# Third feed-forward weights transformed in the prologue and the first batch instead of the last batch of attention

## What is computed

```python
up_gate = jnp.einsum('bsd,hd->bsh', x, W1)
up_lin = jnp.einsum('bsd,hd->bsh', x, W3)
hidden = jax.nn.silu(up_gate) * up_lin
hidden = fwht(hidden)                      # h = 1, 2, 4 ... 512: (a + b, a - b), scale 1/sqrt(1024)
out = jnp.einsum('bsh,dh->bsd', hidden, W2)
...
x = x + _L0_attn_a_ref(_layernorm(x, axis=-1), ...)
x = x + _L0_ffn_ref(_layernorm(x, axis=-1), W1, W2, W3)
x = x + _L0_attn_b_ref(_layernorm(x, axis=-1), ...)
x = x + _L0_ffn_ref(_layernorm(x, axis=-1), W1, W2, W3)
```

## Time and profile before

| | us |
|---|---|
| median of 3 runs | 581.48 (581.45 to 582.91) |
| the profiled execution | 581.49 |
| its span, first to last instruction | 579.7 |
| prologue, up to the first step of `score_kq` | 0 to 35.4 |
| first, second, third, last batch of attention | 35.4 to 87.3, to 141.8, to 196.4, to 248.5 |
| the rest | 248.5 to 579.7 |

### The profile page before, as it was taken

The page is one execution under the profiler, slowest core; times in us unless marked ns, Lnnn a source line. Parts: engine busy times, 40 slices in busy tenths (PEclk is TensorE's granted clock), DMA queues, the critical chain, the costliest instruction groups (busy, mean ns, idle before and its releaser), DMA issues.

```text
span 579.7 us, 8904 instructions
## 1 busy us (share of the span) xinstructions
PE 560.9 (97%) x3278; PEld 388.5 (67%) x3278; DVE 384.3 (66%) x734; ACT 304.5 (53%) x559; POOL 174.1 (30%) x203
## 2 busy tenths in 40 slices
PE   8999999999999989899999999999999999999997
PEld 5543433354344333288889888888778888888887
DVE  6998888988898898754363544458887436354433
ACT  3668778868876877643334342344445333424221
POOL 4453265453344597411101010023333010101000
PEclk9999999999999999999999999999999999999999
DMA  5367320320132310010000000000000010010101
GB/s 155 101 203 209 113 75 30 126 69 1 57 119 90 146 38 3 2 73 1 1 0 1 1 1 2 1 1 0 1 1 1 1 36 1 0 37 2 36 1 37
DMA packets 17995, 25.74 MB, mean 44 GB/s; under 512 B 3048, under 2 KB 11240, under 8 KB 17568
## 3 DMA queue, kind: packets, MB, share of 16 engines
q1 hardware_dynamic: 16732, 24.10, 12.9%
q10 hardware_dynamic: 1220, 1.07, 0.6%
HBM read 10.89 MB, written 5.24 MB: 28 GB/s over the span
## 4 chain that ended last, share of the span: by engine, by line
PE 82%; DVE 8%; ACT 5%; issue 2%; DMA 1%; POOL 1%; ACTq 1%; SPq 0%; DVEq 0%
PE PS L372 80%; DVE mxr L1042 2%; PE PS L383 2%; DVE ring L1132 1%; DMA qf<-in_wq 1%; ACT xTh L787 1%; DVE PR L1243 1%; ACT xf L787 1%; ACT qf L801 1%; DVE XNs L1023 1%; ACT PR L969 1%; POOL xTl L1274 1%; PE PS L588 1%; DVE AOl L1034 1%; DVE OT L1109 0%
## 5 line engine op out<-in xcount | busy, mean ns | idle before, releaser
L372 PE MATMUL PS<-xTh,ring 128*128 128x512 f32 x608 | 188.7, 392 | 0.0
L1042 DVE TENSOR_REDUCE mxr<-PS 128x1 f32<-128x512 f32 x256 | 163.2, 681 | 24.4 <-PE PS L372 23.9
L906 ACT ACTIVATE PR<-PS 128x512 f32<-128x512 f32 x256 | 138.4, 603 | 41.6 <-PE PS L372 41.4
L372 PEld LDWEIGHTS PS<-xTh,ring 128*128 128x128 f32 x608 | 113.2, 188 | 23.6 <-issue 1.7
L372 PE MATMUL PS<-xTl,ring 128*128 128x512 f32 x304 | 110.3, 391 | 0.4 <-POOL xTl L1274 0.4
L372 PE MATMUL PS<-ring 50*128 50x512 f32 (+1 forms) x512 | 99.4, 451 | 5.7 <-DVE mxr L1042 4.4
L1192 DVE TENSOR_TENSOR PR<-PR,PS 128x512 f32<-128x512 f32 x64 | 43.8, 685 | 90.6 <-PE PS L372 66.2
L787 ACT ACTIVATE AOh<-PR 128x512 fp32r<-128x512 f32 x72 | 45.5, 632 | 101.9 <-DVE PR L1192 89.9
L372 PEld LDWEIGHTS PS<-ring 50*128 50x128 f32 (+1 forms) x512 | 41.4, 184 | 83.3 <-ACT PR L906 56.7
L1034 DVE TENSOR_TENSOR AOl<-PR,AOh 128x512 fp32r<-128x512 f32 x72 | 51.1, 710 | 50.3 <-ACT AOh L787 50.3
L1274 POOL TENSOR_TENSOR xTl<-xf,xTh 128x512 fp32r<-128x512 f32 x30 | 43.3, 1459 | 137.0 <-ACT xTh L787 137.0
(11 more groups left out here) (135 smaller groups left out, 627.1 us busy)
## 6 DMA issues: line engine op xcount, KB each, us to landing
ring<-qh SPq DMA_DIRECT2D x48, 128.0 KB, 2.7
ring<-ql SPq DMA_DIRECT2D x24, 128.0 KB, 2.7
ring<-weight_scratch SPq DMA_DIRECT2D x3, 1024.0 KB, 4.7
weight_scratch<-in_w SPq DMA_DIRECT2D x2, 1024.0 KB, 6.8
X<-in_x SPq DMA_DIRECT2D x3, 512.0 KB, 6.7
out<-X SPq DMA_DIRECT2D x6, 256.0 KB, 2.2
ring<-AOh SPq DMA_DIRECT2D x8, 128.0 KB, 2.8
ring<-AOl SPq DMA_DIRECT2D x4, 128.0 KB, 2.8
```

Source lines behind the costliest of these rows:

```text
L372: return nc.tensor.matmul(dst, lhsT, rhs, start=start, stop=stop, skip_group_check=True)
L906: nc.scalar.activation(PR[:, j % 8, :], PS[:, kq_bank(j), :], ACT.Exp, scale=HD ** -0.5)\
L1042: nc.vector.tensor_reduce(mxr[:, S % 2, blk, TT * p + t:TT * p + t + 1], PS[:, QK0 + i % 3, :], AX.X, ALU.max, negate=True).then_inc(max_d ...
```

## The change

1. SyncE loads all of W2 (1 MB) and the Hadamard matrix right after the first small loads, ahead of the bias loads, into the part of X that batches three and four fill later; their own load now waits for the last butterfly (`fly_done` 5).
2. GpSimd runs the first butterfly stage (X into PR) ahead of the splits of the first q and k, the second (PR into X) right behind the first `split_max`, and the third in step 4 of the first batch (into XNs and xf). ScalarE waits for the second stage ahead of its first exponential, since that overwrites PR.
3. The four Hadamard products stand in steps 18, 22, 24 and 28 of the first batch. ScalarE reads each twice (copy into qf, high part into W2h) and GpSimd subtracts. The second half of the v projection of the second batch goes whole into step 26; GpSimd's normalising of the third batch now waits for the first two products.
4. In the last batch products, butterflies and their splits are gone; GpSimd's `output_lo` goes from step 13 back to step 6.
5. In the prologue the first transpose of maxima moves from the front of unit 9's projection to the end of unit 8's (the ninth unit), and the last filler matmul goes. VectorE takes the second batch's statistics in one piece.

```diff
-HAD_AT = (16, 17, 26, 28)
-FLY_AT = (3, 5, 7, 9, 11)
+HAD_AT = (18, 22, 24, 28)
+V_FIRST_AT = ((20,), (26,))
...
@@ sync: behind the loads of rbias
+            sp.dma_start(X[:, 2 * TT:4 * TT, :], w2.rearrange("(f p) n -> p f n", p=P)).then_inc(w2_in, DMA)
+            sp.dma_start(had[:, :], had_d).then_inc(w2_in, DMA)
             sp.dma_start(bvt[:, :], bv.partition_broadcast(P)).then_inc(const_in, DMA)
...
                     if b == 0 and s == 9:
+                        sp.wait_ge(fly_done, 5)
                         for c in range(2, BATCH):
...
@@ tensor: beside_maxima
-                    if U == 9:
+                    project_v(0, (U - 6) // 2, U % 2, PS[:, V_BANK[(U - 6) // 2], :])
+                    if U == 8:
                         pe.wait_ge(ml_done, 1)
...
-                    project_v(0, (U - 6) // 2, U % 2, PS[:, V_BANK[(U - 6) // 2], :])
...
-                else:
+                elif U == 10:
                     keep_busy(1, PS[:, 0, :], FILL)
@@ tensor: shared_bank
+                        elif b == 0:
+                            pe.wait_ge(w2h_done, 4)
...
-                if not more and s in HAD_AT:
+                if b == 0 and s in HAD_AT:
                     j = HAD_AT.index(s)
                     if j == 0:
                         pe.wait_ge(fly_done, 5)
+                        pe.wait_ge(qk_f, 4)
+                    elif j == 1:
                         pe.wait_ge(mt_ready, turned // 8)
                     elif j == 2:
-                        pe.wait_ge(x_done, 2 * b)
+                        pe.wait_ge(w2h_done, 2)
                     else:
-                        pe.wait_ge(w2h_done if j == 1 else w2l_done, j)
+                        pe.wait_ge(v_copied, 4)
                     mm(MB, had[:, :], fly_half(j // 2)[:, j % 2 * SEQ:(j % 2 + 1) * SEQ], True, True)\
                         .then_inc(had_ready, 1)
...
+                if b == 0 and s == V_FIRST_AT[1][0]:
+                    pe.wait_ge(w2h_done, 3)
+                    for part in range(2):
+                        project_v(1, 1, part)
...
@@ scalar
+            act.wait_ge(fly_done, 4)
             for K in range(STEPS * BATCH):
...
-                if b == BATCH - 1 and s in HAD_AT[:2]:
+                if b == 0 and s in HAD_AT:
                     j = HAD_AT.index(s)
                     act.wait_ge(had_ready, j + 1)
-                    hi(hadamard_part(j), MB, 1.0 / HID ** 0.5)
+                    act.wait_ge(*((qk_lo, 7 + j) if j < 2 else (w2l_done, j - 1)))
+                    hi(qf[:, j % 2, :], MB, 1.0 / HID ** 0.5)
                     hi(W2h[:, 2 * j:2 * j + 2, :].rearrange("p f n -> p (f n)"), MB, 1.0 / HID ** 0.5)\
                         .then_inc(w2h_done, 1)
@@ vector
-                if b == BATCH - 1 and s in [k + 1 for k in HAD_AT[2:]]:
...
-                    nc.vector.scalar_tensor_tensor(l, MB, 1.0 / HID ** 0.5, h.bitcast(F32), ALU.mult, ALU.subtract)\
-                        .then_inc(w2l_done, 1)
@@ gpsimd
+            pool.wait_ge(w2_in, 2 * DMA)
+            for h in range(2):
+                v, w = (u.rearrange("p (m u n) -> p m u n", u=2, n=D) for u in (fly_raw(h), fly_near(h)))
+                fly(v[:, :, 0, :], v[:, :, 1, :], w[:, :, 0, :], w[:, :, 1, :])
             first_lo(2)
             first_lo(3)
             split_max(0)
+            for h in range(2):
+                pool.wait_ge(fly_done, h + 1)
+                v, w = fly_near(h), fly_raw(h)
+                fly(v[:, 0:SEQ], v[:, SEQ:], w[:, 0:SEQ], w[:, SEQ:])
...
+                if K == 4:
+                    pool.wait_ge(lnT_ready, 4)
+                    pool.wait_ge(x_hi, 4)
+                    pool.wait_ge(fly_done, 4)
+                    fly(fly_raw(0), fly_raw(1), fly_half(0), fly_half(1))
...
+                        if b == 0:
+                            pool.wait_ge(had_ready, 2)
```

More of the change, by code:

```diff
@@ L146, in build @@
             sem(n) for n in ("wv_in", "wo_in", "bias_in", "ident_in", "const_in", "ones_in"))
-        w2_in = [sem(f"w2_in{h}") for h in range(2)]
+        w2_in = sem("w2_in")
         one_done, zero_done, vone_done, pool_init, whi_done, wlo_done, wol_done = (
@@ L617, in shared_bank @@
                     else:
-                        pe.wait_ge(w2h_done, 2)
+                        pe.wait_ge(mt_ready, turned // 8)
                     for part in range(2):
@@ L628, in shared_bank @@
                     else:
-                        pe.wait_ge(qk_f, 4)
+                        pe.wait_ge(w2h_done, 1)
                     for part in range(2):
                         project_v(b + 1, 0, part)
-                if s in V_AT[1] and more:
-                    if s == V_AT[1][0] and b:
+                if b == 0 and s == V_FIRST_AT[1][0]:
+                    pe.wait_ge(w2h_done, 3)
+                    for part in range(2):
+                        project_v(1, 1, part)
+                if b and s in V_AT[1] and more:
+                    if s == V_AT[1][0]:
                         pe.wait_ge(x_done, 2 * b)
-                    elif s == V_AT[1][0]:
-                        pe.wait_ge(mt_ready, turned // 8)
                     project_v(b + 1, 1, V_AT[1].index(s))
@@ L800, in qk_evacuate @@
                 act.wait_ge(qk_lo, 4 * b + n - 1)
+                if b == 2 and n < 2:
+                    act.wait_ge(w2l_done, 3 + n)
                 nc.scalar.activation(qf[:, n % 2, :], MB, ACT.Identity, bias=bqk[:, n:n + 1]).then_inc(qk_f, 1)
@@ L919, in _ @@
                     for half in range(2):
-                        if s == V_AT[half][-1]:
+                        if s == (V_AT if b else V_FIRST_AT)[half][-1]:
                             v_evacuate(b + 1, half)
-                if b == BATCH - 1 and s in HAD_AT[:2]:
+                if b == 0 and s in HAD_AT:
                     j = HAD_AT.index(s)
                     act.wait_ge(had_ready, j + 1)
-                    hi(hadamard_part(j), MB, 1.0 / HID ** 0.5)
+                    act.wait_ge(*((qk_lo, 7 + j) if j < 2 else (w2l_done, j - 1)))
+                    hi(qf[:, j % 2, :], MB, 1.0 / HID ** 0.5)
                     hi(W2h[:, 2 * j:2 * j + 2, :].rearrange("p f n -> p (f n)"), MB, 1.0 / HID ** 0.5)\
@@ L1083, in _ @@
             dve.wait_ge(x_in[1], DMA)
-            for t in range(2):
-                tile_statistics(TT + t, TT + t)
+            for t in range(TT):
+                last = tile_statistics(TT + t, TT + t)
+            last.then_inc(bst_done, 1)
             stack_rows(0)
             stack_rows(1)
-            for t in range(2, TT):
-                last = tile_statistics(TT + t, TT + t)
-            last.then_inc(bst_done, 1)
             moments(TT, TT, 2)
@@ L1388, in _ @@
                     divide(K // 8 - 1)
-                if s == (13 if b == BATCH - 1 else 6) and b:
+                if s == 6 and b:
                     output_lo(2 * b)
@@ L1404, in _ @@
                        WOh[:, :, :].rearrange("p g n -> p (g n)")).then_inc(wol_done, 1)
[L1405 to L1429 removed]
+                if K == 4:
[3 more added lines that the diff above has]
+                    fly(fly_raw(0), fly_raw(1), fly_half(0), fly_half(1))
+                if b == 0 and s in [k + 1 for k in HAD_AT]:
                     j = HAD_AT.index(s - 1)
                     pool.wait_ge(w2h_done, j + 1)
[L1432 removed]
+                    lo(W2l[:, 2 * j:2 * j + 2, :].rearrange("p f n -> p (f n)"), qf[:, j % 2, :],
                        W2h[:, 2 * j:2 * j + 2, :].rearrange("p f n -> p (f n)")).then_inc(w2l_done, 1)
```

44 lines of the change are left out of this document (4 added, 40 removed).

## The result

| | median of runs, us | lowest to highest | profiled execution | its span | TensorE's clock in it |
|---|---|---|---|---|---|
| before | 582.19 (4 runs) | 581.45 to 582.91 | 581.49 | 579.7 | 1.00 |
| changed | 578.12 (4 runs) | 577.90 to 578.27 | 578.27 | 576.4 | 1.00 |

The ratio is 0.9932 with a 95% interval of 0.9916 to 0.9948: faster by 4.1 us, more than the 0.3% that counts here. The forecast was 578.7. Between the two profiled executions it is 3.2 us.

What follows compares the result with a forecast made beforehand. TensorE, busy 97% of the span, was taken as the bound, so time could come only from its waits. Terms -0.5 + 3.1 - 5.4 = -2.8 us took 581.5 to 578.7 us, range 577.2 to 580.6.

Steps and rivals of the forecast that it cites:

- Part 1: Prologue: the earlier transpose of maxima starts step 0 0.5 us sooner, -0.5 us, bounds 0 and 0.9.
- VectorE allows 0.4 to 0.5: Prologue: VectorE, taking 20 maxima in 13.16 us without a gap, leaves room for a 0.4 to 0.5 us gain.
- The cover for the butterflies: Prologue: W2 lands at 16, GpSimd's idle time from 19.2 hides the butterflies, cost 0.
- the broad reading of the port rule: Prologue: VectorE and GpSimd always exclude each other, so eight butterflies hold maxima up by as much as 10 us.
- Part 2: First batch: four added products cost 4.4 us, waits of 1.31 absorb part, +3.1 us, bounds 2.4 and 4.4.
- step 28's small wait: First batch: step 29's transpose waits about 0.4 us for step 28's copy, given back by small gaps ahead of transposes.
- rival A: First batch: shared-bank hand-overs and ScalarE's copies delay exponentials and eat the gain, 581.0 or half, 580.0; chance 0.20.
- Each pair stands between two steps' exponentials: First batch: ScalarE's two copies per product, about 0.55 us each, fit between exponentials, except in step 28.
- Part 3: Last batch: without products, maxima and then ScalarE's exponentials pace it, -5.4 us, bounds -3.9 and -6.0.
- Rival D: First and last batch: TensorE's 4.4 us only change place, only waits go, 578.5; shares chance 0.58 with the forecast.
- Rival B: Prologue: late W2 delays GpSimd's butterflies, costing us for us from a landing at 22, 584.2 at 27.5; chance 0.04.
- the risk 2 in 100: Whole kernel: gaps in TensorE's work drop its clock to half rate; chance 2 in 100.

Runs made afterwards that it cites:

- e1: Kernel before with only the transpose of maxima moved behind unit 8's projection and the last filler removed: 582.38 us median, ratio 0.9993.
- e3: Changed kernel with the four first-batch Hadamard products and ScalarE's copies of them cut to 8 columns: 575.54 us.
- e7: Changed kernel with the four products at full size and only ScalarE's copies of them cut to 8 columns: 577.54 us.
- e9: Changed kernel with the last product in step 27 instead of 28: 577.83 to 578.64 us at full clock (seven executions), three slower up to 585.22.
- e2: Kernel before without the last batch's four Hadamard products, their copies and splits: 576.15 us.
- e5: Kernel before with one unused Hadamard product added ahead of TensorE's long wait in step 28 of the last batch: 581.51 us.
- e8: Changed kernel with three unused additions on GpSimd ahead of the first butterfly: 580.35 us median.
- e4: Changed kernel with the four products cut to 8 columns, ScalarE's copies and GpSimd's subtractions at full size: 576.65 us.
- e12: Changed kernel with products in two fp32r passes, the last in step 27, and GpSimd making the last batch's step 26 copy: 577.48 us median.

## Why the prediction was right, and what it missed

**Right as a whole.** 578.7 was forecast, 578.12 measured, 578.27 for the profiled execution against which the sum was made. The three terms came out as -0.3, +2.9 and -5.8, forecast as -0.5, +3.1 and -5.4. The measured terms differ from the forecast by +0.2, -0.2 and -0.4 us; that the first two cancel is luck.

**Part 1, sized 0.2 too large.** The transpose came at 29.94 instead of 29.75, and TensorE's step 0 even 0.69 us earlier than before. The step that was mis-sized is "VectorE allows 0.4 to 0.5": I read VectorE's room from its row up to 34.27 and not from the steps behind. Before, it had 0.40 us of idle time at 34.3; now its 14 maxima run from 30.68 to 39.36 without a gap, the chain of waits goes through them, and by step 4 the shift is down to 0.34 us. e1 shows the same without the rest of the change: its first exponential is 0.69 us earlier (35.25 against 35.94) and that of step 8 only 0.32 (48.18 against 48.50). The cover for the butterflies held as written, and with more room: W2 landed at 14.1 where I took 16 from the row of 6.8 us, and its load took 5.5. The butterflies beside maxima cost VectorE nothing: beside the first stage it made 14 in 9.19 us, 0.66 each as in the earlier trace rows, and beside the second 14 in 8.68, 0.62 each, where the kernel before, from 34.67 on, made 8 in 5.04, 0.63 each. So the row was the right guide, and the broad reading of the port rule was not.

**Part 2, sized 0.2 too large, with a wrong split inside.** From step 8 on the stage grew by 2.9: 2.7 over e3 and the 0.2 by which e3 exceeds the kernel before. The products take 2.0 to 2.2, not 3.1, as they fill more than the 1.31 us that had a row; the copies take 0.6 on top, where I had put them at nothing but step 28's small wait. Of these 0.6 the wait of 0.59 us in step 29 is about all, as e7 shows. e9 adds that this wait can't simply be moved away. So rival A was there in a small way: "Each pair stands between two steps' exponentials" cost nothing that shows for three pairs, and the fourth made the wait that I named, without the gaps that I thought would give it back. The working "a step with a product takes it 1.7 us, so the pair fits" was too easy: the pair takes ScalarE about 1.0 us, and the step's own two exponentials take another 1.0. ScalarE falls behind with each product and, from 67.04 on in the changed kernel, makes four exponentials in a row to come back.

**Part 3, sized 0.4 too small.** e2 shows the same 5.8 us without the rest of the change. Step 24 moved by 2.2 (forecast 2.0), the rest is the tail, 3.6 (forecast 3.4): ten exponentials in 5.00 us where I had taken 0.52 each, ScalarE back to back, TensorE waiting 0.43 and 0.23 for them. ScalarE being next, not VectorE, was right. VectorE's cast in step 19 took 0.42 us where it took 1.40 in the earlier trace rows, as GpSimd's subtraction beside it is gone; the four behind it, mostly beside GpSimd's subtractions, took 1.07 each. The Trainium skill (SBUF — State Buffer, "SBUF: two separate sides") says that one of the two holds the shared port for a whole instruction. The trace agrees: before, the subtraction ran from 227.77 to 229.04, and the cast that started at 227.93 ended at 229.33.

**Rival D** gave nearly the same time by another way, so the time could not part the two. The stages do (its first batch would have grown by 4.4, it grew by 3.2), and so does e2 (its 574.0 against 576.15). **Rival B** was right in mechanism and at most 0.4 us off in its point (21.6 to 22.0 for 22), and never near, as GpSimd starts 5.3 us behind the landing.

**What was missed: the clock.** I wrote that no row was at the lower level, and gave the risk 2 in 100. Both were read off the profiled execution. In three sets of runs the kernel before was executed 57 times: 23 times at full clock (581.18 to 581.99), 33 times at 0.996 or 0.997 (582.78 to 583.58) and once at 0.985 (588.35). In most executions TensorE thus falls to its lower level, 1.2 GHz instead of 2.4; by e1 and e5 it does so behind the waits of steps 26 to 28 in the last batch, and it costs 1.4 us. I had 0.57 + 1.48 us of waits in view, and the spread of 1.46 us between the three runs, and did not connect them. The change takes the waits away and with them the fall: all 9 executions of the changed kernel are at full clock. Like with like the change is worth 581.5 - 578.1 = 3.4 us; against the executions with the fall (median 583.0) it is 4.9; the measured ratio mixes both.

The Trainium skill (TensorE: Matmul & The Clock Gate) ties such falls in its section "HAM oscillation" to long waits of TensorE for data, and in the one behind it, on a second failure mode, to frequent short idle times. The rows of e1 are nearer to the second: none of the waits ahead of its fall is longer than 1.5 us, and the kernel before, which has the same waits, was at a lower mean clock in more than half of its executions.

**What stays open.** The filler behind unit 12 is gone in the changed kernel. Of 73 executions of kernels without it 17 have a mean clock of 0.994 or less, and these are 2.8 to 7.7 us above the fastest of their kernel; of 72 with it, one has. Four of the 17 are of e8, which has a new wait. The nearest pair is e1 and the kernel before, 3 in 10 against 1 in 57, and these differ in the place of the transpose as well. The changed kernel itself has none in 9, e4 has 3 in 10 and e9, which differs from it by one step of one product, 3 in 10. In the profiled executions of e9 and e12 the clock falls at about 37 and 37.5 us and stays at 0.50 for about 7 and 10 us. Windows of e9:

```profile
32.00:36.00 4.00, 3.80 (x18) 1.79 (x16) 4.00 (x7) 2.74 (x5) 4.00 (x5) 1.00 0.46 142
36.00:40.00 4.00, 3.90 (x15) 2.06 (x15) 3.15 (x6) 3.21 (x7) 3.92 (x7) 0.62 0.49 156
```

TensorE was busy 3.80 us of 4.00 ahead of that fall, so it is no wait that a row shows. That the filler prevents it is argued from the counts alone; no run had it put back. With 9 executions the changed kernel may well have a fall that was not seen.

## What to carry to other kernels

Move work out of a stage in which it is waited for into one in which TensorE waits for another engine, where it can cost less than its length (here 4.2 us of products cost 2.0 to 2.2) and free more than its length in the stage that it leaves (here 5.8). Then look which engine is next at both places, over the steps behind the edit and not at it alone. When a kernel's runs fall into two levels, put the mean granted clock beside each time first: a wait costs its own length, and the slower clock behind it may cost as much again (here 1.48 and 1.4 us).

## What the runs showed of the hardware

- A clock fall behind short waits (e1): TensorE busy 1.54 us of 3.00, then at 0.50 of full clock from about 243.2 to 246.7, 1.4 us lost. One added product of 1.12 us in the wait, which nobody reads, kept the clock up in 11 of 11 executions.
- The same kernel code but for one step of one product (e9) gave a lower mean clock in 3 of 10 executions, 2.8 to 7.4 us above the fastest. In the one that was profiled the clock fell at 37 us, with TensorE busy 3.80 us of 4.00 ahead of it.
- A VectorE cast of 128x512 takes 0.42 us alone and 1.07 to 1.40 beside GpSimd's subtractions; a maximum over 512 values read from PSUM takes 0.62 to 0.66 with GpSimd's butterflies beside it and without.
- An fp32 product of 128x512 by 128x128 takes 1.06 us on TensorE from start to start, two fp32r passes 0.66. Cut to 8 columns the fp32 product still takes 0.32.
